# Three norms and a mean square moved to ScalarE in a two-layer transformer, with a respread front chain and aligned loops

## The chip, the cores and the metric

One core of one Trainium2 chip runs the kernel. The metric is the device time of one execution in microseconds (us), median of several runs.

## What is computed

Two layers on x of 32 x 256 x 128 (block, token, feature), float32. Each layer is an attention pass and a routed expert pass, each behind a layer norm that is modulated by rows of a small product `mod`, and each added back with a gate:

```python
h = _layernorm(x, axis=-1) * (1 + ca) + sa
x = x + ga * _L1_attn_ref(h, ...)      # layer 1: normalises h once more, and adds that xn to its output
h = _layernorm(x, axis=-1) * (1 + cb) + sb
x = x + gb * _L1_ffn_ref(h, ...)
# in _L1_attn_ref, on h:
    mu = jnp.mean(x, axis=-1, keepdims=True)
    var = jnp.mean(jnp.square(x - mu), axis=-1, keepdims=True)
    xn = (x - mu) * jax.lax.rsqrt(var + LN_EPS) * scale + bias
# in _L1_ffn_ref, on h:
    ms = jnp.mean(x * x, axis=-1, keepdims=True)
    xn = x * jax.lax.rsqrt(ms + EPS) * rms_w
```

Attention has 16 heads of 8 features, layer 0 with a distance bias. The expert pass picks 2 of 8 experts for a token in layer 0 and 1 of 8 in layer 1. Layer 0 has the same two outer norms and neither the inner norm nor the mean square.

## The kernel before, in words

Each layer is an attention program (`attention`) and an expert program (`experts`). The attention program goes over the 32 blocks of 256 tokens (2 tiles of 128 rows, `NT`). It is a software pipeline: tick i works on blocks i+3 (loads) down to i-3 (routing), and `at(off)` in the code is block i+off. There are 38 ticks, i = -3 to 34. `run_ticks` writes the first six and the last six out and puts the 26 between them (i = 3 to 28) in a loop of 13 rounds of two ticks. Every engine has its own program and its own such loop, and they meet only in semaphores. Within an engine the order of the steps in `tick` is the order in its queue, written out by hand; an engine that waits holds all that stands behind it.

What a tick does, in TensorE's order: scores of head 0 to 15 of block i for the row maxima (`scores_a`, into two PSUM buffers A in turn; VectorE's `row_max`, line 867, reads each), and between them eight chunks of two heads of block i-1 (`scores_b`, line 1146), which ScalarE exponentiates (`exps`, line 720), four weighings with the values (`weigh`, line 1161), the projections, transposes (`turn`, line 1092) and the routing products. Scores of head h wait for the maximum of head h-2. The maxima, negated and split in two bf16 halves by `split_max` (lines 874 and 875), are transposed (`turn_max`, line 1133), copied by ScalarE (`max_rows`, line 713) and sent by a DMA (line 526) into the operand of the next chunk 0. `turn_max` for heads 0 to 7 stands behind the scores of head 15 and waits for `pos_read`, which VectorE's `place` gives (line 1006).

The norms. VectorE takes mean and variance (`moments`: two `bn_stats`, two `bn_aggr`, lines 817 and 808), ScalarE makes the inverse root of a column pair with a logarithm and an exponential (`rsqrt_of`, lines 666 and 667), and VectorE applies both to two tiles of 128 columns (`normed`, line 822). In layer 0 this is done for block i+2 (`first_*`) and for block i-2 behind the residual (`second_*`). In layer 1 block i+2 has a longer front chain: GpSimd adds the expert outputs to x (`add_experts`, lines 602 to 604, block i+3), then statistics (`added_stats`), `outer_norm`, two modulating operations (`modulate_rows`, lines 850 and 852), statistics again (`inner_stats`), `inner_norm`, and TensorE's transpose. For block i-2 there are `residual` (line 916), `second_stats`, `second_norm`, GpSimd's `modulate` (lines 616 and 618), `rms_moments` (lines 938 to 941) and `rms_norm` (lines 947 and 949), the last step of VectorE's tick.

VectorE's steps share one helper, `Chain`: `link` and `settle` make an instruction wait until those before it are done, and `meanwhile` puts the next head's maximum into such a wait, for the heads in `MIDST` and in layer 1 alone. GpSimd's tick is: split q and k of block i+1 in parts (lines 592 to 595), `gate_values` (line 609), `modulate`, `scatter` (line 629, indirect DMAs that wait for `slot_in`, line 1014), `add_experts`.

## Time and profile before

| | us |
|---|---|
| median of 3 runs | 2246.19 (2245.32 to 2248.29) |
| the profiled execution | 2240.77 |
| its span, first to last instruction | 2239.0 |
| PE (TensorE) busy | 1779.3, 79% |
| DVE (VectorE) busy | 1652.0, 74% |
| ACT (ScalarE) busy | 1039.1, 46% |
| POOL (GpSimd) busy | 881.2, 39% |

Roughly: 0 to 60 us set-up, 60 to 825 attention of layer 0, 825 to 1160 experts, 1160 to 1970 attention of layer 1, the rest experts. In the rows PEld is TensorE's loading of weights, SPq the queue of SyncE, POOLq and DVEq sequencers. "Idle before" is the time for which an engine had nothing to run before an instruction, and the name behind the arrow is what ended it. An engine's busy share over the span is a mean over these stages; the rows below are of one stage or one tick.

### The profile page before, as it was taken

The page shows a single profiled execution, that of the slowest core. Times are in us where ns is not written, and L with a number is a line of the kernel's source. Part 1 is how long each engine was busy: PE and PEld are TensorE (multiplying, and loading weights), DVE is VectorE, ACT ScalarE, POOL GpSimd, SP SyncE. Part 2 cuts the span into 40 slices and gives each one's busy share as a digit, 9 for nine tenths or more (in the row PEclk, how much of TensorE's full clock was granted, in tenths as well). Part 3 has the DMA queues.
Part 4 walks back from the last instruction along what each step waited for, and adds up shares of the span by engine and source line. Part 5 has one row for each costly group of instructions (what it writes and reads, how often), then busy time and mean ns, then how long its engine had stood idle before and what let it go on. Part 6 is the DMA issues. An engine that isn't in the chain of part 4 may idle for free. (4 is left out here: it accounts for less than half of the span.)

```text
span 2239.0 us, 57857 instructions
## 1 busy us (share of the span) xinstructions
PE 1779.3 (79%) x15650; PEld 1283.3 (57%) x15650; DVE 1652.0 (74%) x5861; ACT 1039.1 (46%) x1967; POOL 881.2 (39%) x932
## 2 busy tenths in 40 slices
PE   2599999999999947999935777777777878719997
PEld 1366666666666727999822444444444444417775
DVE  3488888888888855666626899899898888724453
ACT  0266666666666632222212555555555655603322
POOL 0224444444444333444423444444444444203333
PEclk9999999999999978999966999999999998959999
DMA  3343444343444323222235545545555454243332
GB/s 119 50 65 71 71 70 72 71 70 71 72 71 71 67 52 74 68 68 67 65 121 82 100 98 107 102 99 106 101 102 107 97 102 101 59 146 92 96 93 63
DMA packets 266022, 189.09 MB, mean 84 GB/s; under 512 B 25896, under 2 KB 256202, under 8 KB 265246
## 3 DMA queue, kind: packets, MB, share of 16 engines
q1 hardware_dynamic: 250602, 153.34, 34.7%
q0 software_dynamic: 15360, 35.03, 5.4%
q8 instruction: 28, 0.46, 0.1%
q14 instruction: 32, 0.26, 0.1%
HBM read 93.27 MB, written 53.18 MB: 65 GB/s over the span
## 5 line engine op out<-in xcount | busy, mean ns | idle before, releaser
L867 DVE TENSOR_REDUCE mx<-A 128x2 f32<-128x512 f32 x1024 | 691.8, 682 | 132.2 <-PE A L1126 52.8
L720 ACT ACTIVATE probs<-B 128x1024 f32<-128x1024 f32 x512 | 524.5, 1024 | 380.0 <-PE B L1146 195.5
L1122 PE MATMUL A<-stack 126*128 126x256 bf16 x2048 | 433.2, 283 | 136.2 <-DVE mx L867 102.5
L1146 PE MATMUL B<-stack 128*128 128x256 bf16 x2048 | 357.7, 277 | 32.6 <-DMA stack<-mrow 32.4
L1122 PEld LDWEIGHTS A<-stack 126*128 126x128 bf16 x2048 | 182.0, 99 | 296.8 <-DVE mx L867 213.9
L1161 PE MATMUL M<-probs,vals 128*32 128x256 f32 x4096 | 286.7, 396 | 22.0 <-DVE On L893 16.7
L629 POOL DMA_INDIRECT gathered<-h,slot_in x192 | 187.4, 976 | 154.4 <-DVE slot_in L1014 108.8
L1146 PEld LDWEIGHTS B<-stack 128*128 128x128 bf16 x2048 | 197.2, 101 | 84.3 <-issue 30.6
L616 POOL TENSOR_TENSOR h<-xn,back_rows 128x256 f32<-128x256 f32 x64 | 46.4, 726 | 498.9 <-DVE xn L822 498.9
L1562 PE MATMUL A<-w2s,hid 128*128 128x128 f32 x1792 | 230.4, 278 | 9.1 <-issue 9.1
L1562 PEld LDWEIGHTS A<-w2s,hid 128*128 128x128 f32 x1792 | 211.8, 192 | 18.4 <-issue 13.4
L1553 PE MATMUL B<-xtT,w1s 128*128 128x256 f32 x896 | 215.2, 393 | 5.3 <-DVE xtT L1439 2.0
L1368 POOL DMA_INDIRECT expert_out<-yt,row_dest x144 | 138.4, 961 | 175.4 <-DVE yt L1474 141.1
L1126 PE MATMUL A<-dist,slope_ident 128*128 128x128 bf16 x1024 | 200.6, 221 | 0.0
L1553 PEld LDWEIGHTS B<-xtT,w1s 128*128 128x128 f32 x896 | 167.4, 194 | 39.8 <-issue 16.4
L1161 PEld LDWEIGHTS M<-probs,vals 128*32 128x32 f32 x4096 | 124.9, 111 | 103.9 <-issue 33.9
L1149 PE MATMUL B<-dist,slope_ident 128*128 128x128 bf16 x1024 | 183.5, 219 | 0.0
L1522 ACT ACTIVATE hid<-B 128x1024 f32<-128x1024 f32 x72 | 73.8, 1024 | 226.6 <-PE B L1553 226.6
L592 POOL TENSOR_TENSOR parts<-qk,ones_col 128x512 bf16<-128x512 f32 x64 | 66.5, 1039 | 256.2 <-ACT qk L698 116.4
L1365 POOL DMA_INDIRECT out<-yt,row_dest x80 | 84.6, 1058 | 170.5 <-DVE yt L1479 147.0
L727 ACT ACTIVATE heads<-M 128x256 f32<-128x256 f32 x256 | 98.2, 384 | 106.3 <-PE M L1161 105.8
L1526 ACT ACTIVATE hid<-B,b 128x256 f32<-128x256 f32 x160 | 62.8, 475 | 174.0 <-PE B L1553 138.0
(192 smaller groups left out, 2980.0 us busy)
## 6 DMA issues: line engine op xcount, KB each, us to landing
stack<-parts SPq DMA_DIRECT2D x768, 64.0 KB
xt<-gathered SPq DMA_DIRECT2D x112, 132.0 KB, 2.2
probs<-gathered SPq DMA_DIRECT2D x40, 256.0 KB, 2.7
w<-in_w SPq DMA_DIRECT2D x4, 2048.0 KB
back_rows<-mod_rows SPq DMA_DIRECT2D x64, 128.0 KB, 3.3
x_mid<-X SPq DMA_DIRECT2D x64, 128.0 KB, 1.9
Y<-expert_out SPq DMA_DIRECT2D x64, 128.0 KB
X<-in_x SPq DMA_DIRECT2D x32, 128.0 KB, 3.0
```

The lines of the kernel that those rows point to most:

```text
L629: pool.indirect_dma_start(gathered[l], bass.IndirectOffsetOnAxis(ap=slot_in[u][:, c, t:t + 1], axis=0), (h3 if l else h2)[u][:, t, :], Non ...
L720: act.activation(probs[c % 4][:, :, :, :], Bp[c % 2][:, :, :, :], ACT.Exp, scale=EXP_SCALE[l][c // 4]).then_inc(b_exp.handle, 1)
L727: act.activation(heads[g % 2][:, :], M1[:, 0:S], ACT.Copy).then_inc(o_read.handle, 1)
L867: dve.tensor_reduce(mx[u][:, h, :], A[h % 2][:, :, :], AX.X, ALU.max).then_inc(a_max.handle, 1)
L1122: ins = pe.matmul(A[h % 2][:, t, :], stack[u][0:n, h, 0, t * P:(t + 1) * P], stack[u][0:n, h, 1, :], start=True, stop=(l == 1))
L1126: ins = pe.matmul(A[h % 2][:, t, t * P:(t + 1) * P], slope_ident[:, h % HH, :], dist[:, t, :], start=False, stop=True)
L1146: ins = pe.matmul(Bp[c % 2][:, j, t, :], stack[u][:, h, 1, t * P:(t + 1) * P], stack[u][:, h, 0, :], start=True, stop=(l == 1))
L1149: ins = pe.matmul(Bp[c % 2][:, j, t, t * P:(t + 1) * P], slope_ident[:, h % HH, :], dist[:, 1 - t, :], start=False, stop=True)
L1161: ins = pe.matmul(M1[VW * j:VW * j + VW, 0:S], vals[u][:, t, 4 * g + j, :], probs[(2 * g + j // 2) % 4][:, j % 2, t, :], start=(t == 0), s ...
L1368: ins = pool.indirect_dma_start(expert_out[l], dest, yt[u][:, t, :], None)
L1553: ins = pe.matmul(dst[:, f, :], w1s[u][:, f * P:(f + 1) * P], xtT[u][:, :], start=True, stop=True)
L1562: ins = pe.matmul(A[u][:, t, 0:D], hid[u][:, f, t * P:(t + 1) * P], w2s[u][:, f, :], start=(f == 0), stop=(l == 0 and f == FC - 1))
```

## The change

Seven edits:

1. Layer 0: `first_norm`, and layer 1: `outer_norm` and `inner_norm`, go from VectorE to ScalarE, as an Identity activation with a scale column `rs` and a bias column `shift` per tile. VectorE makes `shift` = -mean * rs with one small instruction (`first_shift`, `inner_shift`).
2. Layer 1: `rms_moments` goes from VectorE. ScalarE squares each tile with a running sum (`rms_of`), and makes the root from the sum.
3. ScalarE's tick is reordered: in layer 1 `first_rsqrt` comes before chunk 2, `outer_norm` before chunk 3, `inner_rsqrt` before chunk 6; `inner_norm` and `rms_of` stand between `head_sums` and chunk 7. `max_rows(0, 0)` now stands ahead of `head_sums(-1, 2)`, in both layers.
4. VectorE's tick in layer 1 is reordered: `added_stats` before heads 2 and 3, `first_shift` behind `normalise(-2, 3)`, `modulate_rows` before head 8, `inner_stats` before head 9, `second_norm` before head 11, `inner_shift` behind it.
5. The counts of order marks per tick change (`DVE_MARKS`, and 5 and 3 to 9 and 4 on ScalarE).
6. The loop over tick pairs is made by `loop_of`: its first instruction is loaded at slot 0 of an instruction fetch block, and a prefetch hint is given for the branch back.
7. Three small buffers are added.

```diff
-DVE_MARKS = (36, 41)
+DVE_MARKS = (35, 33)
...
+def loop_of(eng, rounds):
+
+    return eng.bass.Fori(0, rounds, engines=bass.OrderedEngineSet([eng.engine]), head_slot={eng.engine: 0},
+                         hint_back_edge=True)
...
-    with eng.Fori(0, pairs) as k:
+    with loop_of(eng, pairs) as k:
...
+            def rms_of(b, k, u):
+                act.wait_ge(h2_ready.handle, h2_ready.after(b))
+                for t in range(NT):
+                    ch.link(act.activation(squares[:, :], h2[u][:, t, 0:D], ACT.Square, accum_out=rms[:, t:t + 1]))
+                ch.link(act.activation(rs2[:, :], rms[:, :], ACT.Ln, scale=1.0 / D, bias=eps_col[:, 1:2]))
+                act.activation(rs2[:, :], rs2[:, :], ACT.Exp, scale=-0.5).then_inc(rms_rsqrt.handle, 1)
+
+            def norm_rows(b, k, u, x, ready, sig):
+                act.wait_ge(ready.handle, ready.after(b))
+                act.wait_ge(xn_T.handle, xn_T.after(b - 2))
+                for t in range(NT):
+                    ins = act.activation(xn[u][:, t, :], x[u][:, t, :], ACT.Identity, bias=shift[u][:, t:t + 1],
+                                         scale=rs[u][:, t:t + 1])
+                    if t < NT - 1:
+                        ch.mark(ins)
+                ins.then_inc(sig.handle, 1)
...
                 chunk(0)
                 step(head_sums, -2, 3)
                 step(second_h, -3)
                 layer(0, first_rsqrt, 2)
                 chunk(1)
                 step(read_qk, 1)
+                layer(1, first_rsqrt, 2)
                 chunk(2)
-                layer(1, first_rsqrt, 2)
                 step(max_rows, -1, 1)
                 step(head_sums, -1, 0)
+                layer(1, outer_norm, 2)
                 chunk(3)
...
                 step(head_sums, -1, 1)
+                layer(0, first_norm, 2)
                 chunk(5)
                 step(weights, -3)
                 layer(0, second_rsqrt, -2)
+                layer(1, inner_rsqrt, 2)
                 chunk(6)
-                layer(1, inner_rsqrt, 2)
-                layer(1, rms_rsqrt_of, -2)
+                step(max_rows, 0, 0)
                 step(head_sums, -1, 2)
-                step(max_rows, 0, 0)
+                layer(1, inner_norm, 2)
+                layer(1, rms_of, -2)
                 chunk(7)
                 step(first_h, 2)
...
+            def shift_of(b, k, u, ready, sig):
+                dve.wait_ge(ready.handle, ready.after(b))
+                dve.scalar_tensor_tensor(out=shift[u][:, :], in0=mv[u][:, :, 0], scalar=-1.0, in1=rs[u][:, :],
+                                         op0=ALU.mult, op1=ALU.mult).then_inc(sig.handle, 1)
...
                 maxima(1, 1)
                 layer(0, first_stats, 2)
+                layer(1, added_stats, 2)
                 maxima(2, 2)
-                layer(0, first_norm, 2)
-                layer(1, added_stats, 2)
+                layer(0, first_shift, 2)
                 maxima(4, 1)
                 step(normalise, -2, 3)
+                layer(1, first_shift, 2)
                 maxima(5, 1)
                 step(read_logits, -3)
                 layer(1, residual, -2)
                 maxima(6, 1)
                 layer(0, choose_first, -3)
                 layer(1, second_stats, -2)
-                layer(1, outer_norm, 2)
                 maxima(7, 1)
                 step(split_max, 0, 0)
+                layer(1, modulate_rows, 2)
                 maxima(8, 1)
                 step(normalise, -1, 0)
-                layer(1, modulate_rows, 2)
+                layer(1, inner_stats, 2)
                 layer(1, gated_base, 0)
                 maxima(9, 1)
                 layer(0, choose_second, -3)
                 layer(1, choose_first, -3)
                 maxima(10, 1)
                 layer(0, residual, -2)
-                layer(1, inner_stats, 2)
+                layer(1, second_norm, -2)
                 maxima(11, 1)
                 layer(0, second_stats, -2)
-                layer(1, second_norm, -2)
+                layer(1, inner_shift, 2)
                 maxima(12, 1)
                 step(normalise, -1, 1)
                 step(weigh_choices, -3)
                 maxima(13, 1)
-                layer(1, rms_moments, -2)
                 step(place, -3)
                 maxima(14, 1)
                 layer(0, second_norm, -2)
-                layer(1, inner_norm, 2)
                 maxima(15, 1)
                 layer(1, rms_norm, -2)
```

## Rows read from the trace of the kernel before

**Rows 1.** Stages of layer 0 and layer 1: us, then each engine's busy time.
```profile
140.00:820.00 680.00, 627.28 (x6874) 458.49 (x6871) 581.78 (x1983) 418.02 (x773) 289.51 (x297) 0.99 0.40 69
...
1250.00:1880.00 630.00, 487.92 (x4257) 287.61 (x4256) 562.42 (x1953) 368.54 (x741) 283.28 (x317) 0.96 0.51 103
```

**Rows 2.** Waits, 1300 to 1850 us: total us, times, longest.
```profile
PEld A L1122 <- DVE mx L867: 102.4, 140, 1.4
```

**Rows 3.** Timeline, VectorE, layer 1, running count: start us, duration, instruction.
```profile
1492.46 0.16 DVE L1006 TENSOR_TENSOR run<-run,M 128x8 f32<-128x8 f32 x1
...
1516.49 0.16 DVE L1006 TENSOR_TENSOR run<-run,M 128x8 f32<-128x8 f32 x1
...
1540.10 0.16 DVE L1006 TENSOR_TENSOR run<-run,M 128x8 f32<-128x8 f32 x1
```

**Rows 4.** Timeline, VectorE, one tick of layer 1.
```profile
1500.01 0.69 DVE L867 TENSOR_REDUCE mx<-A 128x2 f32<-128x512 f32 x1 [0.62 <-PE A L1122]
1500.62 0.24 DVE L808 BATCH_NORM_AGGREGATE mv<-st 128x2 f32<-128x6 f32 x2
...
1505.21 1.10 DVE L822 TENSOR_SCALAR xn<-X,mv,rs 128x128 f32<-128x128 f32 x2
...
1508.81 0.68 DVE L867 TENSOR_REDUCE mx<-A 128x2 f32<-128x512 f32 x1
...
1514.74 0.49 DVE L938 BATCH_NORM_STATS2 st<-h 128x6 f32<-128x128 f32 x2
...
1516.28 0.17 DVE L1004 TENSOR_TENSOR rt<-M,run 128x16 f32<-128x16 f32 x1
...
1517.05 0.60 DVE L822 TENSOR_SCALAR xn<-xn,mv,rs 128x128 f32<-128x128 f32 x2
...
1518.16 0.28 DVE L947 TENSOR_SCALAR h<-h,rs 128x128 f32<-128x128 f32 x1
...
1519.19 0.69 DVE L867 TENSOR_REDUCE mx<-A 128x2 f32<-128x512 f32 x1
...
1523.85 0.69 DVE L867 TENSOR_REDUCE mx<-A 128x2 f32<-128x512 f32 x1 [0.61 <-PE A L1122]
```

**Rows 5.** Timeline, VectorE and ScalarE, layer 0.
```profile
503.76 0.64 DVE L822 TENSOR_SCALAR xn<-X,mv,rs 128x128 f32<-128x128 f32 x2
504.97 0.69 DVE L867 TENSOR_REDUCE mx<-A 128x2 f32<-128x512 f32 x1 [0.56 <-PE A L1126]
...
515.55 1.02 ACT L720 ACTIVATE probs<-B 128x1024 f32<-128x1024 f32 x1 [0.95 <-PE B L1149]
```

**Rows 6.** Timeline, TensorE, layer 1.
```profile
1516.78 0.27 PE L1133 MATMUL M<-ident_b,mneg 128*16 128x128 bf16 x2 [0.90 <-DVE run L1006]
...
1520.45 1.07 PE L1161 MATMUL M<-probs,vals 128*32 128x256 f32 x16
```

**Rows 7.** Timeline, ScalarE, layer 1.
```profile
1511.03 1.02 ACT L720 ACTIVATE probs<-B 128x1024 f32<-128x1024 f32 x1 [1.92 <-PE B L1146]
...
1516.40 0.29 ACT L666 ACTIVATE rs<-mv,eps_col 128x2 f32<-128x2 f32 x1 [1.48 <-DVE mv L941]
1516.72 0.20 ACT L667 ACTIVATE rs<-rs 128x2 f32<-128x2 f32 x1
...
1517.17 0.37 ACT L713 ACTIVATE mrow<-M 16x256 bf16<-16x256 bf16 x1
```

**Rows 8.** Groups by line, whole span: busy us, mean ns, idle before.
```profile
L696 ACT ACTIVATE qk<-M,qs_bias,q_scale 128x256 f32<-128x256 f32 x32 | 18.1, 565 | 2.8 <-PE M L1104 2.8
```

**Rows 9.** Timeline, GpSimd and VectorE, layer 1.
```profile
1520.30 0.74 POOL L602 TENSOR_TENSOR Y<-Y 128x256 f32<-128x256 f32 x1
...
1521.93 0.73 POOL L604 TENSOR_TENSOR X<-X,Y 128x256 f32<-128x256 f32 x1
...
1525.57 1.17 POOL L593 TENSOR_TENSOR rem<-qk,parts 128x512 f32<-128x512 f32 x1
1525.85 1.17 DVE L916 TENSOR_TENSOR h<-On,xb 128x256 f32<-128x256 f32 x1
```

More of the change, by code:

```diff
@@ L185, in build @@
         xn = [sb(f"xn{u}", [P, NT, D]) for u in range(2)]
+        shift = [sb(f"shift{u}", [P, NT]) for u in range(2)]
+        squares = sb("squares", [P, D])
+        rms = sb("rms", [P, NT])
         hT = [sb(f"hT{u}", [P, S]) for u in range(2)]
@@ L413, in attention @@
         "before_tri ones_b rev_iota mod_rows gathered x_view region_row".split())
-    gate_rows, ga_rows, wv_ga, wv_id = (g[n] for n in "gate_rows ga_rows wv_ga wv_id".split())
+    gate_rows, ga_rows, wv_ga, wv_id, shift, squares, rms = (g[n] for n in
+        "gate_rows ga_rows wv_ga wv_id shift squares rms".split())
     gb_row, ones_col, Y, expert_out, XR, a, w1, w2, b1, b2 = (g[n] for n in
@@ L803, in _, with moments @@
                 ch.link(dve.tensor_copy(run[:, :], region_row[:, :]))
-            def aggregate(st, mv, sig=None):
+            def moments(x, st, mv, sig):
+                for t in range(NT):
+                    ch.mark(dve.bn_stats(st[:, t, :], x[:, t, :]))
                 ch.settle_apart()
@@ L808, in aggregate, with first_shift, inner_shift @@
                     ins = dve.bn_aggr(mv[:, t, :], st[:, t, :])
[L809 removed]
+                    if t < NT - 1:
                         ch.mark(ins)
                 ch.settle()
[L812 to L818 removed]
+                ins.then_inc(sig.handle, 1)
+            def shift_of(b, k, u, ready, sig):
+                dve.wait_ge(ready.handle, ready.after(b))
+                dve.scalar_tensor_tensor(out=shift[u][:, :], in0=mv[u][:, :, 0], scalar=-1.0, in1=rs[u][:, :],
+                                         op0=ALU.mult, op1=ALU.mult).then_inc(sig.handle, 1)
+            def first_shift(b, k, u):
+                shift_of(b, k, u, rsqrt, shifted)
+            def inner_shift(b, k, u):
+                shift_of(b, k, u, h_rsqrt, h_shifted)
             def normed(x, mv, rs, dst, sig):
@@ L932, in second_norm @@
                 normed(x1_of(u), mv2, rs2, xn2, xn2_ready)
-            def rms_moments(b, k, u):
-                dve.wait_ge(h2_ready.handle, h2_ready.after(b))
-                for t in range(NT):
-                    ch.mark(dve.bn_stats(st2[:, t, :], h2[u][:, t, 0:D]))
-                aggregate(st2, mv2)
-                ch.link(dve.tensor_tensor(mv2[:, :, 0], mv2[:, :, 0], mv2[:, :, 0], ALU.mult))
-                dve.tensor_tensor(mv2[:, :, 1], mv2[:, :, 1], mv2[:, :, 0], ALU.add).then_inc(rms_stats.handle, 1)
             def rms_norm(b, k, u):
```

42 lines of the change are left out of this document (14 added, 28 removed).

## The prediction

> **What bounds the kernel now.** I read the stages first: the attention pass of layer 0 and that of layer 1 are the long ones, with the two expert passes behind them, which the change does not touch. In layer 0 TensorE is busy 627 of 680 us, VectorE 582. In layer 1 TensorE falls to 488 of 630 and VectorE leads with 562 [rows 1]. Then the waits of layer 1: the score matmuls' weight loads stand 102 us behind the row maxima of VectorE in 23 ticks [rows 2]. So layer 0 is near TensorE's own pace and layer 1 is paced by VectorE's queue. Third, the time from tick to tick, read from the running count that VectorE updates once per tick: 24.03 and 23.61 us in turn, mean 23.82 [rows 3]. Last, one tick of layer 1 in order of time, on all engines. I count from T0, the start of the inner norm at 1517.05, right behind the last instruction of `place` [rows 4].
>
> From T0 to the fifth maximum (head 4) the tick takes 6.80 us (1517.05 to 1523.85). From head 4 to the next T0 it takes 17.04 (1500.01 to 1517.05) [rows 4]; there VectorE hardly pauses.
>
> **Layer 0.** Taken off VectorE: two normalising instructions, 0.64 us, once per tick. But the next maximum then waits 0.56 us for TensorE [rows 5]. Without the norm it waits 1.1 less the new shift, and starts when it did. ScalarE gets the two instructions ahead of the exponential of chunk 5, and there it waits 0.95 us for TensorE [rows 5]; that pause takes them in (two norms, 0.87 us, below). Over the stage ScalarE is busy 418 of 680 us [rows 1], so `max_rows` ahead of `head_sums` finds room too. I count zero for layer 0, with bounds of 0.3 us per tick either way (9 us over 30 ticks), should that cover be gone.
>
> **Layer 1, what VectorE loses.** In the stretch from head 4 to T0: the aggregation pair that moves ahead of it, 0.24; the outer norm, 1.10; the second moment, from its first statistics at 1514.74 to the first instruction of `place` at 1516.28, 1.54 less one maximum inside it of 0.61 (1500.01 to 1500.62), so 0.93. Sum 2.27 [rows 4]. Added: two shift instructions on 2 columns, 0.15 each, as small ones of 0.16 in the same rows. 17.04 - 2.27 + 0.30 = 15.1 us. Behind T0 the inner norm goes, 0.51.
>
> **Layer 1, what comes in at T0.** `rms_norm` is the last step of VectorE's tick and waits for a root that ScalarE now makes itself, behind four other steps: `max_rows`, `head_sums`, `inner_norm`, `rms_of`. The first of these waits for the transposed maxima, which TensorE makes only once `pos_read` is given, at 1516.49 + 0.16, T0 - 0.40; the row of the transposes shows them waiting for just that [rows 3, 6]. In the kernel before, the copy of the transposed maxima ran at T0 + 0.12 and the root had been made ahead of it (1516.40 to 1516.92) [rows 7].
>
> Prices on ScalarE. A 256-column pass with two column operands is 0.565 [rows 8]; 1024 columns without any 1.02; 2 columns 0.20 [rows 7]. So a column costs (1020 - 200)/1022 = 0.8 ns, and a norm of 128 columns 0.46, bounds 0.34 (VectorE's price for it) and 0.565. Two back to back take 0.87. The square with its row sum is not in the trace; without the sum it would be 0.20 + 0.10 = 0.30, and the reading of the sum may cost another small pass, 0.20: bounds 0.20 and 0.50, I take 0.35, since the nearest row is that small pass. Logarithm and exponential are 0.29 + 0.20 with 0.06 between them. From T0: maxima copied by 0.5, head sums by 0.85, two norms by 1.7, two squares by 2.4, root by 3.0. VectorE has only the last maximum (0.6) to do in that time. So it stands some 2.4 us, as much as the change takes away from it. Behind the waiting `rms_norm` stand the split of the maxima, head 0, normalise, head 1; TensorE waits for head 0 and for normalise, which in the kernel before released the weighing at T0 + 3.40 [rows 6].
>
> By the Trainium skill, page ScalarE: Activation LUTs, section Rules for kernel authors, plain multiplications and additions belong on VectorE; the page's 186 ns + 0.833 ns a column + 93 ns for each column operand gives 0.48 for one norm, an estimate from that page, against the 0.34 that VectorE's rows show. It speaks against the move and changes the sum by 0.04 us only.
>
> **Then GpSimd.** Its three additions for block b+3 start at T0 + 3.25 and end at T0 + 5.61 (1520.30 to 1522.66) [rows 9]. A VectorE instruction on two SBUF inputs that meets a GpSimd pass stands until it ends: the residual starts at 1525.85, beside GpSimd's of 1525.57 to 1526.74, and is over at 1527.02, 0.28 behind it; with 1.17 us it is longer than the two norm passes of layer 0 together (0.64) for the same 256 columns [rows 5, 9]. The two `rms_norm` instructions started at T0 + 1.1, 0.28 us each, ahead of the additions [rows 4]; at 3.0 they and the two of the split walk into the additions. If the second `rms_norm` stands until 3.99, and the first of the split until 4.80, the other slips into the gap and head 0 starts at 5.1 (before: 2.14) [rows 4]. If every one is caught, 5.85. If none is, 4.1.
> The Trainium skill, GPSIMD Engine Reference, section Specifications, says that GpSimd shares its SBUF interface with VectorE and is in contention with instructions that have two SBUF inputs or a 2-port mode; by that rule both halves of `rms_norm` and the split are exposed, and the residual's row agrees (1.17 us).
>
> From head 0 TensorE's own order sets the time to head 4: weighing, transposes, heads 2 and 3, the projections, head 4. In the kernel before these took 3.4 us from the weighing at T0 + 3.40 to head 4 at 6.80; with normalise and head 0 in front of the weighing, 4.45 from head 0. So head 4 starts at 9.5 (5.1 + 4.45), against 6.80.
>
> **One more new wait.** `inner_shift` follows head 11 on VectorE and needs `inner_rsqrt`, which sits behind exponential 5 on ScalarE. Head 9 ended at 1509.5; the exponential ran 1511.03 to 1512.05 [rows 4, 7]; with the routing exponential (0.21) and the root (0.55) that is 3.3 us behind head 9. VectorE needs some 2.6 for head 10 (0.6), the seven steps of the choice (0.2 each), half of the second norm and head 11 (0.6). It stands 0.7. Bounds 0 and 1.0. For first shift and the split caught in GpSimd's four passes I add 0.2. The added statistics now come before head 2, at some T0 + 7; the additions are done at 5.61, so no wait. The front loads on SP stand behind the stacking DMAs that need the split; they start later in the tick by as much as the tick grows and still land in time.
>
> Tick of layer 1: 9.5 + 15.1 + 0.7 + 0.2 = 25.5 us, +1.66 against 23.84 (1500.01 to 1523.85) [rows 4]. Thirty ticks have both the maxima and the second moment: +50 us.
>
> **Loops.** A back edge stands between every second pair of ticks. In layer 1 the interval from 1492.46 to 1516.49 has one in it and is 0.42 us longer than the next [rows 3]. Twelve times that is 5 us, if the edge is all of the difference, and as much in layer 0 at most; the hint is itself an instruction, and the entry into each loop gets a branch. I take -3, bounds -10 and +3.
> The Trainium skill, Runtime: NRT & Kernel Launch, section Instruction fetch mechanics, says that a taken branch to a page not at hand stalls for a fetch. The rows show at most 0.42 us of that, and by the page the hint would be worth no more than this.
>
> **Sum.** The profiled execution is 2240.8 us (span 2239.0 and 1.8 around it), the median 5.4 above it. 2246.2 + 50 - 3 = 2293.
>
> **Rivals.**
> Not caught (20 in 100): the wait at `rms_norm` is there, the additions catch nothing. Head 4 at 8.55, tick 8.55 + 15.1 + 0.7 = 24.35: +15 - 3, 2258. For it: GpSimd's additions wait for loads that may land later. Against: they start a fixed 3.1 us behind `slot_in`.
> All caught (12): head 0 at 5.85 and the inner shift caught too, tick 26.3: +74 - 3, 2317.
> The other side (22): ScalarE's chain is shorter and the time taken from VectorE counts. It decides at the root: if it is there by T0 + 2.2, `rms_norm` and the split (0.5 each) are over by 3.2, before the additions at 3.25; head 4 at 7.65, tick 7.65 + 15.1 = 22.75 with the inner wait hidden: -33 - 3, 2210. For it: copies of the maxima now come first on ScalarE; norms at VectorE's 0.34 and squares at 0.20 give 2.2. Against: two column operands and the row sum both cost in the rows.
> No effect (8): ticks stay within 0.15 us, as TensorE's order absorbs both signs: 2246.
>
> **How the numbers follow.** The forecast has 38 in 100: slower. With all caught and most of not caught: slower 0.66; the other side and the low tail of the forecast's bounds give faster 0.24; same 0.10, where 0.2% (4.5 us) is about what a measurement can tell. The range reaches from the other side to all caught: 2208 to 2322.
>
> **What would show it.** VectorE's wait at `rms_norm` for ScalarE, near 2.4 us in each tick of layer 1; `rms_norm` or the split longer than 0.3 us with a GpSimd addition beside them; head 4 near T0 + 9.5; the stretch behind it near 15.9; layer 0's stage as long as before. I am wrong if the root is there before the last maximum is done, or if the layer-1 tick is under 23.6.

## The result and the profile after

| | before | after |
|---|---|---|
| median | 2247.24 us (2245.32 to 2249.80) | 2373.97 us (2372.28 to 2375.55) |
| ratio, 95% interval | | 1.0569 [1.0553, 1.0585] |
| profiled execution | 2240.77 us (span 2239.0) | 2375.55 us (span 2373.7) |
| a tick of layer 0 | 22.52 us | 23.18 us |
| a tick of layer 1 | 23.84 us | 27.33 us |
| VectorE busy, of the span | 1652.0 us, 74% | 1626.0 us, 68% |

The direction was forecast and the size was not: 127 us slower, where 47 were forecast. A tick here is the mean of 25 intervals between the updates of the running count, once a tick, as in [rows 3]. With them the spans' difference of 134.7 us divides into: layer 1's 25 steady intervals +87.3, layer 0's +16.5, the last ticks of each loop and the drain behind it +8.5 in layer 0 and +12.1 in layer 1, the stretch between the two attention passes +9.0, the end +1.3.

The page's head, and busy time by stage (columns as in [rows 1], the last three being TensorE's granted clock, the transfers' share, and GB/s):

```profile
span 2373.7 us, 57948 instructions
...
PE 1839.7 (78%) x15650; PEld 1314.9 (55%) x15650; DVE 1626.0 (68%) x5573; ACT 1118.1 (47%) x2287; POOL 883.4 (37%) x932
```
```profile
140.00:820.00 680.00, 622.44 (x6741) 449.41 (x6741) 574.32 (x1885) 422.53 (x805) 278.07 (x285) 0.99 0.36 67
1290.00:1975.00 685.00, 503.97 (x4025) 299.02 (x4025) 515.49 (x1653) 394.07 (x901) 272.42 (x300) 0.88 0.42 90
```

In layer 1 no engine is near its limit any more: VectorE, 89% busy before, is at 75%, and TensorE's granted clock went from 0.96 [rows 1] to 0.88. Time in which an engine does nothing has come in. One tick of layer 1 on VectorE shows where (start, duration, instruction, idle time ahead of it and what ended it). I count T0 as in the prediction, from right behind `place`: 1641.00 here.

```profile
1640.44 0.16 DVE L1024 TENSOR_TENSOR run<-run,M 128x8 f32<-128x8 f32 x1
...
1641.50 0.69 DVE L894 TENSOR_REDUCE mx<-A 128x2 f32<-128x512 f32 x1 [0.40 <-PE A L1139]
1644.51 0.56 DVE L965 TENSOR_SCALAR h<-h,rs 128x128 f32<-128x128 f32 x1 [2.33 <-ACT rs L693]
1645.11 0.75 DVE L967 TENSOR_SCALAR h<-h,rs 128x128 f32<-128x128 f32 x1
...
1645.98 0.63 DVE L902 SCALAR_TENSOR_TENSOR mneg<-mx,mneg 128x16 bf16<-128x16 f32 x1
1646.53 0.68 DVE L894 TENSOR_REDUCE mx<-A 128x2 f32<-128x512 f32 x1
...
1650.75 0.69 DVE L894 TENSOR_REDUCE mx<-A 128x2 f32<-128x512 f32 x1 [1.43 <-PE A L1139]
1652.41 0.69 DVE L894 TENSOR_REDUCE mx<-A 128x2 f32<-128x512 f32 x1 [0.97 <-PE A L1139]
...
1667.79 0.16 DVE L1024 TENSOR_TENSOR run<-run,M 128x8 f32<-128x8 f32 x1
```

Line 965 is `rms_norm`: it stands 2.33 us for the root of line 693, and in [rows 4] its like stood for nothing. The waits of VectorE from 1350 to 1950 us say that it does so in every tick (total us, times, longest):

```profile
DVE mx L894 <- PE A L1139: 72.0, 82, 1.5
DVE h L965 <- ACT rs L693: 50.2, 22, 2.3
```

ScalarE's part of the same tick shows who holds the root up. The maxima's copy, the head sums and the inner norm come first, and each square is followed by an instruction of its own that reads the sum:

```profile
1641.79 0.37 ACT L746 ACTIVATE mrow<-M 16x256 bf16<-16x256 bf16 x1 [1.56 <-PE M L1150]
1642.07 0.36 ACT L760 ACTIVATE heads<-M 128x256 f32<-128x256 f32 x1
1642.33 0.86 ACT L699 ACTIVATE xn<-xn,shift,rs 128x128 f32<-128x128 f32 x2
1643.10 0.29 ACT L691 ACTIVATE squares<-h 128x128 f32<-128x128 f32 x1
1643.30 0.18 ACT L691 ACTIVATION_READ_ACCUMULATOR squares<-h 128x1 f32 x1
...
1644.28 0.20 ACT L693 ACTIVATE rs<-rs 128x2 f32<-128x2 f32 x1
```

GpSimd's additions (lines 612 to 614) stand beside the held instructions of VectorE, 1644.51 to 1646.61:

```profile
1644.25 0.73 POOL L612 TENSOR_TENSOR Y<-Y 128x256 f32<-128x256 f32 x1
1645.06 0.72 POOL L613 TENSOR_TENSOR Y<-Y,gb_row 128x256 f32<-128x256 f32 x1
1645.86 0.72 POOL L614 TENSOR_TENSOR X<-X,Y 128x256 f32<-128x256 f32 x1
```

Last, TensorE, and four stretches of the tick (columns as above, the granted clock third from the end):

```profile
1647.27 0.47 PE L1139 MATMUL A<-stack 126*128 126x256 bf16 x2 [1.83 <-DVE mx L894]
1647.73 1.94 PE L1178 MATMUL M<-probs,vals 128*32 128x256 f32 x16
```
```profile
1641.00:1647.30 6.30, 2.94 (x25) 1.64 (x22) 3.50 (x8) 4.93 (x13) 4.14 (x5) 1.00 0.44 121
1647.30:1650.00 2.70, 2.70 (x20) 1.17 (x21) 1.99 (x8) 0.28 (x1) 0.00 (x0) 0.53 0.44 53
...
1652.40:1664.00 11.60, 8.58 (x82) 5.40 (x81) 10.25 (x36) 7.25 (x17) 5.30 (x5) 1.00 0.33 68
1664.00:1668.30 4.30, 3.46 (x29) 1.86 (x29) 4.16 (x16) 1.62 (x5) 1.45 (x2) 0.60 0.64 169
```

TensorE is busy 2.94 of 6.30 us, stands its last 1.83 us for head 0, and comes back at a clock of 0.53, near the lower of its two clock levels (1.2 of 2.4 GHz). The weighing takes 1.94 us in place of 1.07 [rows 6]. The clock is low again at the end of the tick (0.60), behind waits of 1.28 us and less. None of this stood in the forecast. Over 24 steady ticks the tick shown is a typical one: head 0 comes at T0 + 5.34 in the mean, and from head 0 to head 4 it takes 5.92 us at a clock of 0.71; in the kernel before these are 2.31, and 4.62 us at 1.00.

### The profile page after: what moved, and what is told of

It is laid out like the page before. It is cut to its first block and busy times, and to the rows that moved or that the text cites. A ratio compares the mean times of both kernels' runs of the same rounds, so it can differ in the third digit from the quotient of the medians.

```text
span 2373.7 us, 57948 instructions
## 1 busy us (share of the span) xinstructions
PE 1839.7 (78%) x15650; PEld 1314.9 (55%) x15650; DVE 1626.0 (68%) x5573; ACT 1118.1 (47%) x2287; POOL 883.4 (37%) x932
## 5 line engine op out<-in xcount | busy, mean ns | idle before, releaser
L1139 PE MATMUL A<-stack 126*128 126x256 bf16 x2048 | 450.3, 292 | 185.1 <-DVE mx L894 147.7
L1163 PE MATMUL B<-stack 128*128 128x256 bf16 x2048 | 374.0, 287 | 11.9 <-DMA stack<-mrow 10.7
L1139 PEld LDWEIGHTS A<-stack 126*128 126x128 bf16 x2048 | 188.4, 102 | 349.4 <-DVE mx L894 270.3
L1178 PE MATMUL M<-probs,vals 128*32 128x256 f32 x4096 | 312.1, 424 | 54.7 <-DVE On L920 46.6
L1163 PEld LDWEIGHTS B<-stack 128*128 128x128 bf16 x2048 | 208.9, 106 | 66.6 <-issue 16.1
L1178 PEld LDWEIGHTS M<-probs,vals 128*32 128x32 f32 x4096 | 133.0, 118 | 149.8 <-issue 60.5
L1570 PEld LDWEIGHTS B<-xtT,w1s 128*128 128x128 f32 x896 | 168.3, 195 | 40.6 <-issue 16.5
```

Of the source, the lines that this page charges most:

```text
L1139: ins = pe.matmul(A[h % 2][:, t, :], stack[u][0:n, h, 0, t * P:(t + 1) * P], stack[u][0:n, h, 1, :], start=True, stop=(l == 1))
L1163: ins = pe.matmul(Bp[c % 2][:, j, t, :], stack[u][:, h, 1, t * P:(t + 1) * P], stack[u][:, h, 0, :], start=True, stop=(l == 1))
L1178: ins = pe.matmul(M1[VW * j:VW * j + VW, 0:S], vals[u][:, t, 4 * g + j, :], probs[(2 * g + j // 2) % 4][:, j % 2, t, :], start=(t == 0), s ...
L1570: ins = pe.matmul(dst[:, f, :], w1s[u][:, f * P:(f + 1) * P], xtT[u][:, :], start=True, stop=True)
```

## The experiments

Ticks are the means of the same 25 intervals. On three of the chips layer 0's ticks are 26.3 to 27.2 us for every kernel tried there, also for those whose layer 0 is that of before, and the kernel before then takes 2361 to 2377 us in place of 2245; the table's last ten rows are from these. Ratios are always against the kernel before on the same chip.

| kernel | median us | ratio, 95% interval | layer 0 | layer 1 |
|---|---|---|---|---|
| loop_undone | 2352.7 | 1.0477 [1.0460, 1.0495] | 23.16 | 27.36 |
| loop_alone | 2268.0 | 1.0097 [1.0080, 1.0114] | 22.75 | 23.91 |
| square_on_vector | 2340.1 | 1.0410 [1.0382, 1.0439] | 23.14 | 27.10 |
| filler | 2321.8 | 1.0344 [1.0327, 1.0361] | 23.15 | 25.75 |
| root_first | 2262.3 | 1.0067 [1.0050, 1.0083] | 23.15 | 23.92 |
| modulate_later | 2279.7 | 1.0140 [1.0117, 1.0162] | 23.15 | 24.67 |
| layer0_only | 2246.3 | 0.9995 [0.9985, 1.0005] | 22.57 | 23.83 |
| square_filler | 2228.6 | 0.9920 [0.9903, 0.9936] | 23.22 | 23.02 |
| root_used_later | 2376.5 | 1.0076 [1.0053, 1.0099] | 26.43 | 24.72 |
| later_with_filler | 2384.0 | 1.0110 [1.0086, 1.0133] | 26.34 | 24.83 |
| layer0_norm_on_vector | 2449.7 | 1.0389 [1.0365, 1.0412] | 26.50 | 27.36 |
| square_alone | 2347.9 | 0.9948 [0.9932, 0.9964] | 26.65 | 23.89 |
| tiles_alone | 2372.3 | 0.9978 [0.9964, 0.9993] | 27.12 | 23.89 |
| tiles_last | 2378.9 | 1.0007 [0.9995, 1.0019] | 27.09 | 23.94 |
| square_filler_last | 2352.6 | 0.9898 [0.9880, 0.9916] | 27.16 | 23.08 |
| root_first_filler_last | 2369.7 | 0.9967 [0.9950, 0.9983] | 27.06 | 23.71 |
| tiles_alone_again | 2355.9 | 0.9976 [0.9966, 0.9986] | 26.49 | 23.91 |
| square_filler_last_again | 2333.4 | 0.9881 [0.9864, 0.9898] | 26.60 | 23.07 |

**The loop, undone and alone.**

```diff
 # loop_undone, in the changed kernel; loop_alone is the reverse, in the kernel before
-    with loop_of(eng, pairs) as k:
+    with eng.Fori(0, pairs) as k:
```

> The changed kernel with the old loop form, all else kept. Theory A (the exit of the hinted loop makes TensorE stand for code, 3.4 us at 743.9 us, and the clock falls behind it): the ticks 28 to 30 lose their 8 us in layer 0 and 7 us in layer 1, the entry of layer 1 some more; 2355 us, with the steady ticks at 23.2 and 27.3 us as in the changed kernel. Rival B (the aligned loop also sets the phase in which GpSimd meets VectorE's routing steps in layer 0): layer 0 ticks go back to 22.5 us as well, 2340 us or less. If the loop form does nothing: 2374.

> The kernel before with the aligned, hinted loop alone. Theory A: steady ticks as before (22.5 and 23.8 us), two exits at some 5 to 8 us each: 2260 us. Rival B: layer 0 ticks at 23.1 us on top of that, 2275 us. If the hint pays at each back edge of layer 1 (0.4 us, twelve times) it takes 5 us off either.

The loop costs 21 us in the one and 24 in the other, and no steady tick gets shorter by more than 0.03 us; Theory A holds. The largest part of the price lies where the loop is left: by the spans the two kernels differ from their partners by 19.0 and 28.7 us, of which 13.3 and 14.8 lie in the last ticks of the two loops and the drain behind them, and 3.7 and 5.7 between the two passes (in `loop_alone` 5.9 more are in layer 0's steady ticks). TensorE of the changed kernel, at layer 0's exit (the tick around it takes 27.52 us, and 22.15 before):

```profile
743.90 0.37 PE L1139 MATMUL A<-stack 126*128 126x256 bf16 x1 [3.40 <-issue]
...
746.55 1.94 PE L1178 MATMUL M<-probs,vals 128*32 128x256 f32 x16
```

"Issue" means that it waited for nothing that the profile shows, and the weighing behind it takes 1.94 us again. The loop's last branch is recorded at 739.75, ahead of this stop. At layer 1's exit TensorE stands 2.21 us in the same way. With the old loop the ticks around the two exits take 22.34 and 26.96 us, as ordinary ticks do. The trace has 26 prefetch hints on each engine, one for each of the 13 rounds of the two loops, so the last round hints at the loop's head too. That TensorE waits for instructions at the exit fits this and is not shown, and the hint and the alignment were not tried apart. The Trainium skill, Runtime: NRT & Kernel Launch, section Instruction fetch mechanics, says that a taken branch out of the pages at hand stalls for a fetch. It says nothing of a loop's exit or of a hint; the 3.40 us are this trace's.

**The clock.** In `filler`, eight matmuls that only repeat others stand at the head of each tick of layer 1.

```diff
 # filler, in loop_undone's kernel, scores_b
-                for j in range(2):
+                for j in 3 * [0, 1] if l == 1 and c == 0 else range(2):
```

> The changed kernel with the old loop form; in layer 1 TensorE makes the eight products of chunk 0 three times over, into the same places, while it has to wait for head 0 anyway (1.8 us of idle). Eight more matmuls per tick and no work less. Theory D (TensorE's idle behind chunk 0 lets its clock fall to half, which costs 1.4 us per tick between head 0 and head 4): with the idle under 1 us the granted clock there stays at 1.0, weighing takes 1.07 instead of 1.94 us and the tick of layer 1 gets shorter by about 1 us, 30 us in all, against the loop_undone kernel. Rival E (the clock is low for another reason, or does not matter): the same or up to 0.5 us longer per tick.

More work made it 31 us faster, as Theory D said. From 1350 to 1850 us, loop_undone and then filler:

```profile
1350.00:1850.00 500.00, 366.94 (x2944) 217.00 (x2944) 377.46 (x1211) 287.73 (x660) 198.88 (x220) 0.88 0.43 90
```
```profile
1350.00:1850.00 500.00, 372.65 (x3307) 231.24 (x3303) 397.88 (x1279) 310.56 (x706) 213.54 (x235) 0.97 0.45 95
```

The clock goes from 0.88 to 0.97 and a tick from 27.36 to 25.75, 1.61 us of the 3.5 by which layer 1's tick had grown. From head 0 to head 4 the clock is 1.00 in place of 0.71 and the stretch takes 4.55 us in place of 5.92 (means of 24 ticks), so 1.37 of the 1.61 us is the slow clock there; head 0 also comes 0.18 us earlier. The wait at `rms_norm` had to be charged twice. The Trainium skill, TensorE: Matmul & The Clock Gate, section HAM oscillation, describes waits for transfers between bursts of matmuls that leave the next burst on the slow clock. This trace agrees that the burst behind a wait is slow (0.53); the waits of the page's example are longer than the 1.83 us here.

**Who makes the root late.** Three kernels: the root's own operations back on VectorE, its use moved into the next tick, its making moved up on ScalarE. All have the old loop.

```diff
 # square_on_vector: rms_moments on VectorE ahead of place, ScalarE only takes the root
-                layer(1, rms_of, -2)
+                layer(1, rms_moments, -2)
 # root_used_later: on VectorE, from the tick's end to behind head 1 of the next
                 maxima(1, 1)
+                layer(1, rms_norm, -3)
...
-                layer(1, rms_norm, -2)
 # root_first: on ScalarE, from behind inner_norm to ahead of max_rows
                 chunk(6)
+                layer(1, rms_of, -2)
                 step(max_rows, 0, 0)
...
-                layer(1, rms_of, -2)
                 chunk(7)
```

> The changed kernel with the old loop form and with the mean square back on VectorE, its root made on ScalarE ahead of the transposed maxima, as before; the three norms stay on ScalarE. Theory A (the wait of rms_norm for ScalarE, 2.3 us, what it makes VectorE meet in GpSimd's additions, and the slow clock behind it are the loss of layer 1): the tick of layer 1 falls from 27.3 to 22.5 to 23.5 us, at or under the 23.8 of before, although VectorE gets 0.9 us of work back; 2220 to 2250 us. Rival C (the norms on ScalarE and the new waits for them hold the tick): it stays above 25 us, 2290 us or more.

The wait for the root went, but the mean tick is still 27.10 us, which by the numbers is Rival C's side. The ticks alternate between 24.85 and 29.77 us. In the long ones VectorE stands some 3 us at its back edge for nothing that the profile shows (in one the loop's branch is recorded at 1645.65 and the sequencer's next instruction at 1648.60); neither kernel has this (waits from 1350 to 1850 us). In the short ones the statistics of the front chain, now ahead of head 2, wait for GpSimd:

```profile
DVE mneg L897 <- issue: 27.7, 9, 3.2
```
```profile
1625.40 0.48 DVE L839 BATCH_NORM_STATS2 st<-X 128x6 f32<-128x128 f32 x2 [1.43 <-POOL X L614]
```

So this run tells less than I meant it to; of the edit's own effect it shows the short ticks, 2.5 us under loop_undone's 27.36.

> The changed kernel with the loop of before, and with layer 1's scaling of the expert columns by the root (rms_norm) taken from the end of its tick to the next tick, behind head 1's maximum. Nothing is left out. At the tick's end VectorE then has nothing that waits for ScalarE's root. Theory A (the root's wait of 2.3 us lets TensorE stand, its clock falls to half behind it, and the late heads 1 to 4 follow from that): the wait and the slow clock at the tick's end both go, the clock of layer 1 comes back to 1.00, head 0 to head 4 is back at 4.5 us from 5.9; the tick falls from 27.36 by 2.3 and 1.4 and some of the late heads to 23.0 to 24.0 us, and the time from 2352.7 to 2245 to 2270. Rival B (the drift comes from elsewhere: the forward norms on ScalarE and the new places on VectorE, which wait for GpSimd): VectorE's idle time only moves behind head 2 to 4, to the statistics that wait for GpSimd's added rows; the tick stays over 24.8 us, and the time over 2290.

24.72 us, between the two forecasts. The wait at the root is gone, and the clock is 1.00 from head 0 to head 4, but now TensorE stands later in the tick, for the first normalised heads, and the clock falls behind that (TensorE, and the stretch behind it):

```profile
1702.70 1.07 PE L1178 MATMUL M<-probs,vals 128*32 128x256 f32 x16 [1.28 <-DVE On L920]
```
```profile
1705.00:1711.00 6.00, 5.42 (x39) 3.23 (x36) 5.37 (x23) 2.54 (x5) 1.45 (x2) 0.52 0.77 156
```

> The changed kernel with the loop of before, and with the mean square moved up on ScalarE from behind the inner norm to ahead of the transposed maxima. Nothing is left out. Theory A (the root is late because it stands behind the maxima's transposes and the inner norm in ScalarE's order, not because of its own length of 1.4 us): the root ends 1.5 to 2.5 us earlier, VectorE's wait for it falls from 2.3 to under 0.7 us, and layer 1's tick falls from 27.36 to 24.5 to 26.0 us (the held steps of the routing and the late start of the statistics stay). Rival B (the square waits for GpSimd's modulation of the rows, so that it only holds up the maxima and the norm behind it): the wait moves from VectorE to TensorE (maxima and the transposed norm) and the tick stays over 26.5 us.

The widest step of the study: one line moved in ScalarE's order takes the ratio from 1.0477 to 1.0067, some 90 us, and the tick from 27.36 to 23.92, below what I had given it (24.5 to 26.0). ScalarE, then VectorE, the last instruction of `place` starting at 1654.15:

```profile
1652.72 0.30 ACT L691 ACTIVATE squares<-h 128x128 f32<-128x128 f32 x1
...
1653.91 0.20 ACT L693 ACTIVATE rs<-rs 128x2 f32<-128x2 f32 x1
1654.43 0.37 ACT L746 ACTIVATE mrow<-M 16x256 bf16<-16x256 bf16 x1 [0.32 <-PE M L1150]
```
```profile
1654.85 0.28 DVE L965 TENSOR_SCALAR h<-h,rs 128x128 f32<-128x128 f32 x1
1655.16 0.29 DVE L967 TENSOR_SCALAR h<-h,rs 128x128 f32<-128x128 f32 x1
...
1657.02 0.69 DVE L894 TENSOR_REDUCE mx<-A 128x2 f32<-128x512 f32 x1 [0.66 <-PE A L1139]
```

The squares run while ScalarE would stand for the transposed maxima (1.56 us in the changed kernel, 0.32 here), and they need only GpSimd's rows, which are there. `rms_norm` is over at 1655.45, ahead of GpSimd's additions (1657.46), so nothing is held. The whole chain that followed from the late root, the hold and the slow clock from head 0 to head 4, is gone (1.00 in place of 0.71). Over layer 1's steady ticks the clock is still 0.94, and 0.96 in the kernel before.

**What the rest of the edits does in layer 1.**

```diff
 # modulate_later, in root_used_later's kernel
-                layer(1, modulate_rows, 2)
                 maxima(8, 1)
                 step(normalise, -1, 0)
+                layer(1, modulate_rows, 2)
                 layer(1, inner_stats, 2)
```

> root_used_later with the two row operations of the modulation back behind the first normalised heads, where they stood before the change (they were moved ahead of head 8). Nothing is left out. In root_used_later each tick of layer 1 holds a wait of TensorE of 1.28 us for these heads, and the granted clock falls to 0.5 in the 6 us after it in some ticks. Theory A (the respread itself costs this): the wait falls under 0.4 us, the clock stays at 1.00 there, and layer 1's tick falls from 24.72 to 22.8 to 24.0 us. Rival B (VectorE holds the next maximum back by the same work wherever it stands): the tick stays at 24.5 to 25.0.

24.67 against 24.72: rival B. The wait only moved to the next maximum:

```profile
1631.28 0.39 PE L1139 MATMUL A<-stack 126*128 126x256 bf16 x2 [1.80 <-DVE mx L894]
```

`square_alone` puts only `rms_of` into the kernel before, in the place where ScalarE took the root (ahead of the head sums and maxima), and takes the second moment off VectorE; the norms stay there. `later_with_filler` is root_used_later with filler's edit (scoring matmuls, which the expectation below calls transposing ones).

> The kernel before with one part of the change alone: layer 1's mean square on ScalarE (two squares with accumulated sums, logarithm, exponential), VectorE's six operations of it taken out; the three norms, their places and the loop as before. Nothing is left out. Theory A (the root that comes too late is the main loss): VectorE waits 1.0 to 2.3 us for the root at the end of layer 1's tick, TensorE stands over 1 us behind it, and the tick grows from 23.84 to 25.0 to 27.0 us although VectorE has 1.4 us less to do; time 2275 to 2330. Rival B (the root is late only because the inner norm and the reordered maxima stand ahead of it on ScalarE): the wait is under 0.5 us, the tick is 22.5 to 23.6, and the time 2215 to 2240, faster than before. Layer 0 is as before.

> root_used_later with the eight extra transposing matmuls in each tick of layer 1 that the run filler had, at the same place. Nothing is left out of the results. Theory A (without the root's wait the clock doesn't fall any more, so filler has nothing to keep up): within 8 us of root_used_later, the extra matmuls costing 0 to 0.4 us a tick. Rival B (TensorE still stands long enough elsewhere in the tick for its clock to fall): it is 10 to 30 us faster than root_used_later.

`later_with_filler` gains nothing (24.83): where the clock falls at another place of the tick, matmuls at its head are no help. In `square_alone` the root is not waited for, which is Rival B's mechanism, and 0.5% is gained over the whole, but the steady tick is that of before (23.89 against 23.84) and not 22.5 to 23.6. The next run says that the reason is the clock again. Its ticks alternate, and this is the stretch ahead of a long one and its first 5 us:

```profile
1641.00:1646.00 5.00, 3.29 (x35) 1.84 (x32) 4.70 (x15) 2.32 (x6) 1.02 (x2) 1.00 0.45 118
1646.00:1651.00 5.00, 2.93 (x27) 1.64 (x29) 4.83 (x22) 2.98 (x8) 1.45 (x2) 0.86 0.57 123
1651.00:1656.00 5.00, 5.00 (x31) 2.65 (x24) 3.99 (x14) 3.11 (x8) 2.94 (x4) 0.50 0.50 166
```

In the first ten microseconds TensorE was busy 3.29 and 2.93 of 5 us each, with no pause of 0.9 us or more, and the clock began to fall in the second five (0.86). So I put the filler there, behind heads 8 to 15:

```diff
 # square_filler, in square_alone's kernel, scores_b
-                for j in range(2):
+                for j in 2 * [0, 1] if l == 1 and c >= 4 else range(2):
```

> square_alone (the kernel before with the mean square alone on ScalarE) with four extra scoring matmuls in each of the last four score pairs of a tick of layer 1, where TensorE is busy only 58 to 64% of the time; each pair is computed twice into the same place, so the results are the same. In square_alone layer 1's ticks alternate between 22.8 to 23.8 and 24.4 us, and the granted clock is 0.50 for the first 5 us of the long ones. Theory A (TensorE's low load in the second half of the tick costs the clock, and the clock costs the tick): all ticks come to 22.7 to 23.4, layer 1 is 15 to 30 us shorter, and the time is 1.2 to 2% below the kernel before. Rival B (the filler itself delays the maxima): ticks 24.0 to 24.8, slower than square_alone by 5 to 25 us.

The clock is 1.00 in layer 1 and the tick 23.02, the first under before's:

```profile
1350.00:1850.00 500.00, 414.81 (x3841) 267.58 (x3834) 442.92 (x1478) 315.67 (x694) 232.55 (x260) 1.00 0.43 107
```

Both kernels are beaten: 0.9920, short of the forecast 1.2 to 2% since layer 0 lost 0.70 us a tick. The kernel before has a clock of 0.96 there and was not tried with these extra matmuls alone, so how much of the gain needs the mean square on ScalarE is not known.

**Layer 0.** `layer0_norm_on_vector` undoes layer 0's norm in loop_undone's kernel; `layer0_only` makes only that edit in the kernel before; `tiles_alone` allocates the change's four small tiles in the kernel before and uses none.

```diff
 # tiles_alone, in the kernel before
         rs = [sb(f"rs{u}", [P, NT]) for u in range(2)]
+        shift = [sb(f"shift{u}", [P, NT]) for u in range(2)]
+        squares = sb("squares", [P, D])
+        rms = sb("rms", [P, NT])
 # tiles_last, square_filler_last, root_first_filler_last: the new tiles behind Y, the last one
```

> The changed kernel with the loop of before, and with layer 0's first norm back on VectorE at its old place (two passes of 0.3 us behind head 3) in place of the shift and ScalarE's norm. Nothing is left out, and layer 1 is as changed. Theory A (the slower ticks of layer 0, 23.16 against 22.52 us, come from the norm's absence on VectorE, which puts the routing steps beside GpSimd's split, where they are held longer): layer 0's tick falls to 22.5 to 22.7 and the time by 10 to 18 us from 2352.7, to 2335 to 2343. Rival B (the order of the transposed maxima and the head sums on ScalarE, which this run keeps as changed, sets it): layer 0 stays at 23.1 to 23.2 and the time at 2350 to 2355. Layer 1's tick is 27.3 by both.

> The kernel before with one part of the change alone: layer 0's first norm on ScalarE behind head sums 1, VectorE computing the shift in its place; ScalarE's order of the transposed maxima and the head sums, layer 1 and the loop as before. Nothing is left out. Theory A (the norm's move alone puts the routing steps beside GpSimd's split): layer 0's tick grows from 22.52 to 23.0 to 23.3 us, layer 1 stays at 23.84, and the time is 12 to 22 us above the kernel before. Rival B (the order of maxima and head sums on ScalarE does it): layer 0 stays within 0.15 us of 22.52 or gets faster, and the time within 4 us of the kernel before.

> The kernel before with the change's four new on-chip tiles (shift 0 and 1, squares, rms: 536 bytes in each partition) allocated where the change allocates them, and never used; every instruction is that of before, only the addresses of the tiles behind them differ. Nothing is left out. Theory A (the addresses set layer 0's loss): layer 0's tick grows from 22.52 to 23.0 to 23.3 us, the transfers' share of the 16 engines in layer 0 falls from 36% to 26 to 33%, and the time is 12 to 20 us above before. Rival B (it is ScalarE's order of maxima and head sums): layer 0 stays at 22.5, the time within 4 us of before.

> root_first (the changed kernel, loop of before, the mean square moved up on ScalarE) with the four new tiles allocated behind all others, so that every other tile has its address of before. Nothing is left out. Theory A (addresses): layer 0's tick falls from 23.15 to 22.4 to 22.7 us, layer 1's stays near 23.9, and the time falls from 2262 to 2243 to 2250 us, the time of the kernel before. Rival B (ScalarE's order in layer 0): layer 0 stays at 23.15 and the time at 2258 to 2265.

> square_filler (mean square alone on ScalarE, extra matmuls in the last four score pairs of layer 1's tick) with the two new tiles behind all others. Nothing is left out. Theory A (addresses): layer 0's tick falls from 23.22 to 22.5, layer 1's stays at 23.0, and the time falls from 2228.6 to 2208 to 2216 us, 1.4 to 1.7% under the kernel before. Rival B: the time stays within 4 us of 2228.

> tiles_last with the extra matmuls of square_filler. Nothing is left out. Theory A (with the root early and the clock held up, the change's 2.6 us a tick of work taken from VectorE come to count): layer 1's tick is 22.2 to 23.0 us and the time 2195 to 2225 us. Rival B (TensorE's waits for ScalarE's norm, 0.95 us, and for the normalised heads, 1.28 us, bound the tick with the new places of the front chain): the tick stays at 23.4 to 24.0 and the time at 2235 to 2250 us, so the norms' part of the change brings nothing.

> tiles_alone once more: the kernel before with the change's four new tiles allocated and never used. Nothing is left out. Theory A (the addresses of the other tiles set layer 0's loss): layer 0's tick is 23.0 to 23.3 us against 22.52, and the time 12 to 20 us above the kernel before. Rival B (ScalarE's order of maxima and head sums does): layer 0 at 22.5, the time within 4 us of before. If layer 0's tick is over 25 us, the run says nothing on it.

> square_filler_last once more: mean square alone on ScalarE, extra matmuls in the last four score pairs of layer 1's tick, the two new tiles behind all others. Nothing is left out. Theory A (addresses): layer 0's tick is 22.5, layer 1's 23.0, and the time 1.4 to 1.7% under the kernel before. Rival B: layer 0's tick is 23.2 and the time 0.7 to 0.9% under it, as square_filler's.

`layer0_only` settles one half: the move of the norm costs nothing (22.57, ratio 0.9995), as forecast. `square_filler` tells against ScalarE's order as well: its instructions of layer 0 are those of before, and it has the 0.70 us. `layer0_norm_on_vector` ran on a chip of the slow kind and tells nothing of it. What grew is the same in the changed kernel and in square_filler, the routing steps that meet GpSimd's split (busy us, mean ns, idle ahead, from 200 to 640 us), before and then square_filler:

```profile
L958 DVE TENSOR_TENSOR rt<-rev_iota,h 128x16 f32<-128x16 f32 x19 | 14.7, 773 | 0.7
L955 DVE TENSOR_TENSOR rt<-lg,r 128x16 f32<-128x16 f32 x19 | 11.2, 591 | 0.7
...
L980 DVE SCALAR_TENSOR_TENSOR rt<-rt,lg 128x16 f32<-128x16 f32 x19 | 7.7, 403 | 0.0
...
L969 DVE TENSOR_SCALAR h<-token_ids 128x2 f32 x19 | 3.0, 158 | 0.0
```
```profile
L952 DVE TENSOR_TENSOR rt<-lg,r 128x16 f32<-128x16 f32 x19 | 21.6, 1135 | 0.7
...
L955 DVE TENSOR_TENSOR rt<-rev_iota,h 128x16 f32<-128x16 f32 x19 | 13.2, 696 | 0.6
L966 DVE TENSOR_SCALAR h<-token_ids 128x2 f32 x19 | 10.6, 559 | 0.0
...
L977 DVE SCALAR_TENSOR_TENSOR rt<-rt,lg 128x16 f32<-128x16 f32 x19 | 3.2, 166 | 0.0
```

The four take 1.93 us a tick before and 2.56 here: +0.63 of the 0.70. These two kernels differ in layer 0 by the addresses of tiles and by where the program lies. Which of the two shifts the steps against the split, `tiles_alone` and `tiles_last` were to tell, and could not: all runs of them fell on chips where layer 0's tick is 26.5 to 27.1 us and the loss doesn't appear (ratios 0.9978, 0.9976 and 1.0007). That stays open, and so does why layer 0 runs so there. What the traces do show: in all ten kernels run there VectorE stands 3.1 to 3.5 us in the mean, about once a tick of layer 0, ahead of a row maximum, and the end of that wait is put down to "remote", to no instruction of the core; the kernel before has no such wait. Each chip was used on one occasion only, so the chip and the occasion can't be told apart.

`square_filler_last` has the best ratio: 0.9898 and 0.9881, 24 to 29 us under the kernel before. That is less than the forecast 1.4 to 1.7%, and about what layer 1 gives: 0.77 us in each of its ticks. `root_first_filler_last` has all of the change but the new loop, with the root early and the extra matmuls: 0.9967, tick 23.71, slower than without the norms on ScalarE. By the tick Rival B holds. But its clock over those ticks is 0.96 and not the 1.00 of square_filler_last, and the norms' move and the respread of the front chain were not tried apart in it; that the two together brought nothing is shown, and which of them is at fault is not.

## Why the prediction was right or wrong

The direction and the way to it were right: a late root, VectorE's stop at `rms_norm`, GpSimd's hold behind it. The step of the sum that failed is head 0 to head 4 of layer 1, priced at 4.45 us with TensorE at full clock and measured at 5.88. Two more terms were mis-sized, the loops (-3 us, measured +21 to +24) and layer 0 (0, measured 16 to 20).

**The root's wait: right.** Root at T0 + 3.0 and 2.4 us of standing were forecast; it ended at T0 + 3.48 and VectorE stood 2.33. ScalarE's prices held as well: two norms 0.86 (0.87), one square with its sum 0.41 from start to start (0.35), though the sum is read by a second instruction of 0.18. The reason held too: `root_first` changes nothing but the order ahead of the root.

**The hold by GpSimd: right, a little short.** Three instructions of four were caught (0.56, 0.75, 0.63), and head 0 came at T0 + 5.53 for 5.1 (5.34 in the mean of 24 ticks).

**From head 0 to head 4: here it failed.** The 4.45 us were read off [rows 4, 6], where the clock is full (4.62 in the mean of the kernel before). They took 5.88 (1646.53 to 1652.41), since TensorE had stood 1.83 us and came back at 0.53. I had said that TensorE waits for head 0 and had given that wait no price of its own. That the clock can fall was in front of me: layer 1 has 0.96 and layer 0 0.99 in [rows 1]. With the eight extra matmuls of `filler` this stretch takes 4.55 us at a clock of 1.00, so the clock was the cause.

**Head 4 to the next T0: right in size.** 15.1 with 0.9 of waits, 16.0 was forecast, 15.94 measured (1652.41 to 1668.35), but in other parts: the inner shift waits only in 4 ticks of 22, and the last 4.3 us run at 0.60.

So layer 1's tick was 27.33 and not 25.5: over the 25 steady intervals 46 us. With layer 0's 16 and the loop's 24 (21 in place of -3) that is the 81 us by which the forecast was low, within 5; that is an addition of medians and of one execution's ticks, and the forecast had counted thirty ticks where 25 are steady.

**Layer 0, counted as nothing: right for the edit, wrong for the kernel.** The norm's move is free (`layer0_only`). The 0.65 us a tick, 16 to 20 us in all, comes with no instruction of layer 0.

**The loops: wrong in sign.** -3 with bounds of -10 and +3; they cost 21 to 24. I priced the back edge alone. TensorE's stop at the exit, 3.40 us, and the slow clock behind it had no row before, and its bounds should have reached as far up as down.

**The rivals.** The other side's mechanism was sound: it said that the tick decides at the root, with the root there by T0 + 2.2. With `root_first` it is there at T0 - 0.1 (1653.91 + 0.20 against 1654.22), and all the delay goes. But its gain was not: it gave 22.75 us for the tick, and with VectorE's lighter load it is only 23.92. What stands in a tick of it then is TensorE's wait for ScalarE's inner norm (0.95), for the normalised heads (1.28), and VectorE's for GpSimd's additions (up to 1.2); which of them sets the tick was not tried.

The loss adds up in ratios: loop 0.0092 (1.0569 to 1.0477), the root's place 0.0410 (to 1.0067), and what is left, 0.0067, is 15 us, near layer 0's 25 ticks at 0.63.

## What to carry to other kernels

Before a step is moved to an engine that is half idle, look at what stands ahead of it in that engine's order: here the same operations cost 90 us behind three others, the first of which waits, and nothing that can be seen ahead of them. Price a wait of TensorE twice, once for the time and once for the clock behind it, and where the granted clock is under 1.00, try whether a few repeated matmuls in the thin part of a loop pay for themselves: here eight a tick took 1.61 us off one kernel's tick and sixteen 0.87 us off another's, and eight in the wrong place nothing. Price a loop's exit and not only its back edge.

## What the runs showed of the hardware

- A ScalarE instruction on 128 columns with a summed output is two in the trace: 0.29 to 0.31 us and a read of 0.18 to 0.19 (changed kernel).
- The clock fell to half without any long pause: 6.22 of 10 us busy, no pause of 0.9 us, and then 0.50 over 5 us in `square_alone`.
- TensorE stood 3.40 and 2.21 us at the exits of the aligned loops with a hinted back edge (3.04 and 2.97 in `loop_alone`), and not with the old loop. In `square_on_vector`, with the old loop, VectorE stood 2.9 to 3.3 us at every back edge of layer 1.
- A VectorE instruction on 16 columns took 1.14 us in the mean beside GpSimd's split in layer 0 of `square_filler`, nearly as long as the residual's 1.17 us on 256 columns [rows 9].
- The chip, or the occasion, matters: layer 0's tick was 22.5 to 23.2 us on some and 26.3 to 27.2 on others, layer 1's the same on all (23.8 to 23.9 for the same instructions).
